# Another step table for the small stages of an attention, in a kernel of attention and mixture of experts

## The chip, the cores and the metric

The kernel runs on one core of one Trainium2 chip. The metric is the device time of one execution in microseconds (us), as the median of several runs. A core has five engines with an instruction queue each: TensorE (PE in the profile, matrix products and transposes by product; PEld is its weight load), VectorE (DVE), ScalarE (ACT), GpSimd (POOL) and SyncE (SP, which here only issues DMAs). Each engine works through its own queue in order; between engines there are semaphores.

## The reference

Eight batches of 512 tokens of width 512, all in fp32. Latent attention with 16 heads of 32, then routed and shared experts, each between two layer norms:

```python
x = x + layernorm(attention(layernorm(x)))
x = x + layernorm(ffn(layernorm(x)))
# attention: c_kv = x @ W_DKV + b, c_q = x @ W_DQ + b; k_c, v_c from c_kv, q_c from c_q
#            k = [k_c, rope(x @ W_KR)], q = [q_c, rope(x @ W_QR)]
#            ctx = softmax(q k^T / sqrt(32)) v_c; return ctx @ W_O + b_O
# ffn:       router (top 2 of 16 experts), routed relu^2 experts + shared relu^2 expert
```

## The kernel before

The kernel has four stages in a row: attention (to about 960 us), the first half of the shared expert with the routing beside it, the routed experts, and the second half of the shared expert with the combination. The change touches the attention alone.

**Units.** The attention is cut into 32 units `u`. A unit is four heads of one batch: `b = u // 4` is the batch, `g = u % 4` the group, so that each batch has a first (g = 0), second, third and fourth unit. For each unit PE makes 16 tiles of scores of 128 keys by 512 queries (`scores`, L598 and L603, two products into one PSUM bank); ACT takes the exponential of each (L1373) into a ring of eight tiles `K.pt`; PE multiplies four at a time with the values (`values`, L614); POOL adds the last twelve to the first four (`K.acc`, L1570) for the softmax's denominators. The maxima that the softmax needs are taken one unit ahead: PE makes 16 tiles of the next unit's products (`top`, L584) into three PSUM banks, DVE reduces each to its row maxima (L888), and when all 16 are reduced PE transposes them (`rows`, L590), which the next unit's scores need.

**Small stages.** After a unit's last values its context is kept (`keep`, ACT, L1380), `total` sums `K.acc` over partitions (PE, L623), `invert` transposes and inverts it (DVE, L895, L897, L900), `divide` multiplies the context with it (POOL, L1577), `round` makes the context's high part in fp32r (ACT, L1385), and `low` subtracts it from the context, which leaves the low part (DVE, L905, both operands in SBUF, 128x512). These six stages of unit u-1 stand in unit u. Beside them stand the halves of q and k two units ahead (`half`, then `send`, which passes them through DRAM, SP, L1719 to L1729), and by group: in the first unit the transposes of the next batch's input and the last batch's output projection (`project`, DVE L915), in the second the latent projections (`proj`) and the first norm of the last batch's output with four residual additions on POOL (L1604), in the third the rope projection and the second norm, in the fourth the values of the next batch, its norm, and the last batch's routing.

**What sets the order.** `beside_order(u)` gives each stage of a unit a step from 0 to 35 out of the table `STEP`; the sixteen scores stand at the even steps 0, 2, ... 30. All stages are sorted by `(32 * u + step, rank)`, and this one list is the order of instructions of every engine: each engine takes from it the stages that it has work in. There is no other planner. An engine that comes to a stage whose input is not there waits, and all that stands behind it in its queue waits too. Two numbers a stage in the table apart can thus stand close on one engine and far apart on another: `"round1": 24` and `"low1": 18` say that in a second unit DVE's subtraction stands at step 18 and the copy on ACT that it needs at step 24.

Of the kernel before, what the change touches and what calls it, by code (L numbers as in the profile page):

```python
# [137 lines left out]
def before_order(b):  # L138
    return ([("turn", b, k) for k in range(4)], [("proj", b, w) for w in ("kv", "q", "r")], [("v", b, i) for i in range(4)])


STEP = {"last values0": 9, "total0": 8, "invert0": 10, "divide0": 2, "round0": 14, "low0": 15, "k0": 1, "q0": 3, "rows0": 27,
# [10 lines left out]


def beside_order(u):
# [3 lines left out]
    def put(name, items):  # L159
        where = STEP[f"{name}{g}"]  # L160
        at.extend(((32 * u + n, 1), x) for n, x in zip(where if isinstance(where, tuple) else [where] * len(items), items))
# [9 lines left out]
    if u + 1 < NU:  # L171
        due = STEP[f"tops{g}"]
        for n in range(16):
# [1791 lines left out]
```

## Time and profile before

| | |
|---|---|
| three runs | 1722.57, 1723.14, 1726.42 us (median 1723.14) |
| the profiled execution | 1726.61 us, of which the span of the trace is 1724.8 |
| PE busy | 1581.1 us (92% of the span) |
| DVE, ACT, POOL busy | 986.8, 832.1, 795.4 us |
| attention, first exponential to last | 75.5 to 958.6 us |
| the four units of the fourth batch | 36.7, 24.1, 27.2, 28.1 us (second, third, fourth, then the first of the fifth) |

A row of the profile gives an engine, a line of the kernel, output and input by name, the form and how many there are, and behind the bar or in brackets for how long the engine was idle just before and who ended that. Names are those of the memory rooms: `a`, `s`, `c` and `f` are tiles in SBUF, `bank` is PSUM. Times of a timeline are us from the span's start.

### The profile page before, as it was taken

The numbers are of one execution on the slowest core, as the hardware profiler recorded it, in microseconds if no ns is written. First come the engines' busy times: TensorE is split into PE (matmuls) and PEld (weight loads), VectorE is DVE, ScalarE is ACT, GpSimd is POOL, SyncE is SP. The second block draws the span as 40 slices with busy tenths as digits, with TensorE's granted clock in tenths as the row PEclk, the third lists the DMA queues.
The fourth block names the chain that finished last, engine by engine and source line by source line (L and its number), as shares of the span: only waits on it lengthen the run. The fifth ranks groups of instructions, "written<-read, shape, count | busy, mean of one in ns | idle before, by whom it ended". The sixth has DMA issues, their size and how long they took to land.

```text
span 1724.8 us, 22216 instructions
## 1 busy us (share of the span) xinstructions
PE 1581.1 (92%) x7386; PEld 1078.2 (63%) x7386; DVE 986.8 (57%) x1896; ACT 832.1 (48%) x1496; POOL 795.4 (46%) x820
## 2 busy tenths in 40 slices
PE   4799979899899798998997899998999999979997
PEld 3465646556556465564563577887676767657886
DVE  3667677776766776767666442565111111128998
ACT  2356546465475464555654345430333333346554
POOL 1167767666677667666776440002222222122341
PEclk9799999899899899999998999997999999989999
DMA  4747457364384583653752325114833333367773
GB/s 119 209 127 204 113 142 238 98 195 142 122 241 116 138 250 98 180 157 122 214 178 91 122 73 190 48 39 145 317 126 131 126 131 127 118 233 249 231 244 129
DMA packets 123767, 270.57 MB, mean 157 GB/s; under 512 B 15396, under 2 KB 27044, under 8 KB 117508
## 3 DMA queue, kind: packets, MB, share of 16 engines
q1 hardware_dynamic: 97256, 205.97, 39.5%
q0 software_dynamic: 12912, 41.82, 7.6%
q10 hardware_dynamic: 13488, 21.37, 3.4%
q8 instruction: 61, 1.00, 0.2%
q14 instruction: 50, 0.41, 0.1%
HBM read 154.03 MB, written 92.01 MB: 143 GB/s over the span
## 4 chain that ended last, share of the span: by engine, by line
PE 73%; DVE 7%; DMA 7%; issue 5%; ACT 3%; SPq 3%; POOL 2%; DVEq 0%; POOLq 0%; ACTq 0%
PE bank L109 10%; PE bank L699 10%; PE bank L677 8%; PE bank L755 8%; PE bank L778 8%; PE bank L584 6%; PE bank L598 6%; PE bank L614 5%; PE bank L603 5%; DMA a<-kq_scratch 3%; PE bank L738 2%; SPq L1729 2%; DVE a L905 2%; DVE a L888 1%; DMA a<-in_L_attn_x 1%
## 5 line engine op out<-in xcount | busy, mean ns | idle before, releaser
L1570 POOL TENSOR_TENSOR a<-a 128x512 f32<-128x512 f32 x384 | 494.7, 1318 | 102.8 <-ACT a L1373 102.1
L1373 ACT ACTIVATE a<-bank 128x512 f32<-128x512 f32 x512 | 296.0, 597 | 246.0 <-PE bank L603 220.0
L888 DVE TENSOR_REDUCE a<-bank 128x1 f32<-128x512 f32 x512 | 323.3, 681 | 57.2 <-PE bank L584 55.8
L109 PE MATMUL bank<-a 128*128 128x512 f32 (+1 forms) x864 | 241.5, 402 | 6.1 <-DVE a L834 4.0
L598 PE MATMUL bank<-a 128*128 128x512 f32 x512 | 221.5, 433 | 4.6 <-ACT a L1373 4.6
L603 PE MATMUL bank<-a 68*128 68x512 f32 x512 | 205.6, 402 | 0.4 <-ACT a L1363 0.2
L584 PE MATMUL bank<-a 128*128 128x512 f32 x512 | 185.4, 431 | 22.0 <-DMA a<-kq_scratch 16.6
L677 PE MATMUL bank<-c 128*128 128x512 f32 x768 | 185.8, 401 | 19.3 <-ACT c L1425 11.4
L109 PEld LDWEIGHTS bank<-a 128*128 128x128 f32 (+1 forms) x864 | 161.5, 189 | 54.3 <-issue 10.3
L1639 POOL DMA_INDIRECT f<-h_scratch,f x79 | 74.8, 947 | 252.7 <-PE bank L738 230.0
L1211 DVE TENSOR_TENSOR f<-f 128x256 f32<-128x256 f32 x79 | 33.6, 425 | 267.9 <-ACT f L1497 267.9
L677 PEld LDWEIGHTS bank<-c 128*128 128x128 f32 x768 | 147.1, 193 | 56.3 <-issue 12.6
L699 PE MATMUL bank<-c 128*128 128x512 f32 x768 | 176.0, 389 | 2.1 <-ACT c L1440 1.6
L598 PEld LDWEIGHTS bank<-a 128*128 128x128 f32 x512 | 98.2, 192 | 107.5 <-issue 48.5
L699 PEld LDWEIGHTS bank<-c 128*128 128x128 f32 x768 | 143.9, 188 | 33.0 <-issue 2.2
L755 PE MATMUL bank<-f 128*128 x632 | 151.4, 383 | 0.2 <-issue 0.2
L584 PEld LDWEIGHTS bank<-a 128*128 128x128 f32 x512 | 98.4, 197 | 81.2 <-DVE a L888 23.0
L778 PE MATMUL bank<-f 128*128 x316 | 148.5, 593 | 0.0
L614 PE MATMUL bank<-a 128*32 128x512 f32 x1024 | 139.5, 627 | 0.0
L755 PEld LDWEIGHTS bank<-f 128*128 128x128 f32 x632 | 115.1, 192 | 13.6 <-issue 1.0
L905 DVE TENSOR_TENSOR a<-s,a 128x512 fp32r<-128x512 f32 x32 | 93.0, 2907 | 29.2 <-ACT a L1385 29.2
L603 PEld LDWEIGHTS bank<-a 68*128 68x128 f32 x512 | 98.4, 192 | 16.0 <-ACT a L1363 1.2
(186 smaller groups left out, 1904.5 us busy)
## 6 DMA issues: line engine op xcount, KB each, us to landing
a<-kq_scratch SPq DMA_DIRECT2D x192, 256.0 KB, 5.9
kq_scratch<-a SPq DMA_DIRECT2D x32, 1024.0 KB, 4.1
a<-a SPq DMA_DIRECT2D x80, 256.0 KB, 5.4
yp_scratch<-f ACTq DMA_DIRECT2D x79, 256.0 KB, 2.0
a<-in_L_attn_x SPq DMA_DIRECT2D x15, 1024.0 KB, 9.2
x_scratch<-a SPq DMA_DIRECT2D x8, 1024.0 KB, 5.2
h_scratch<-a SPq DMA_DIRECT2D x8, 1024.0 KB, 12.5
hT_scratch<-s SPq DMA_DIRECT2D x8, 1024.0 KB, 7.6
```

The lines of the kernel that those rows point to most:

```text
L109: t = e.matmul(out, a[n], b[n], start=n == 0 and m == 0, stop=n == len(ah) - 1 and m == 2)
L584: e.matmul(MX[n % 3][:], K.Qc[:, z, j, i * P:(i + 1) * P], K.Kc[:, z, j, :], start=True, stop=True).then_inc(Z.top, 1)
L598: e.matmul(SC[n % 2][:], K.Kc[:, z, j, i * P:(i + 1) * P], K.Qc[:, z, j, :], start=True, stop=False)
L603: e.matmul(SC[n % 2][:], K.KR[0:68, b % 2, j, i * P:(i + 1) * P], K.QR[0:68, u % 2, :], start=False, stop=True).then_inc(Z.score, 1)
L614: t = e.matmul(CT[HD * j:HD * j + HD, :], K.v[:, u % VS, i, HD * j:HD * j + HD], K.pt[:, n % NP, :], start=i == 0, stop=i == 3)
L677: t = e.matmul(bank[:], (K.sul if a else K.suh)[:, k, cut], (K.hTl if c else K.hTh)[:, k, :], start=m == 0, stop=m == 11)
L699: t = e.matmul(bank[:], (K.aTl if a else K.aTh)[:, k, cut], (K.sdl if c else K.sdh)[:, k, :], start=m == 0, stop=m == 23)
L755: t = e.matmul(K.UP[z][:, 0:FI], K.hTt[:, z, k * P:(k + 1) * P], K.flat[:, bass.ds(reg[i] + k * FI, FI)], start=k == 0, stop=k == 3)
L778: t = e.matmul(K.DN[z][:], K.eaT[:, z, k * P:(k + 1) * P], K.flat[:, bass.ds(reg[i] + 4 * FI + k * D, D)], start=k == 0, stop=k == 1)
L888: e.tensor_reduce(K.mx[:, i, j:j + 1], K.MX[n % 3][:], AX.X, ALU.max).then_inc(Z.max, 1)
L1373: e.activation(K.pt[:, n % NP, :], K.SC[n % 2][:], ACT.Exp, scale=SCALE).then_inc(Z.exp, 1)
L1570: e.tensor_tensor(K.acc[:, j, :], a, K.pt[:, n % NP, :], ALU.add).then_inc(Z.acc, 1)
```

## The change

86 of the table's 169 numbers change; nothing else is touched, so that each engine has the same instructions with the same operands, in another order. Of the table the rows of the second unit's low part:

```diff
-        "values0": (15, 15, 29), "tops0": (3, 4, 5, 6, 6, 7, 10, 11, 14, 14, 16, 16, 16, 16, 16, 16), "last values1": 7,
-        "total1": 7, "invert1": 7, "divide1": 8, "round1": 24, "low1": 18, "k1": 9, "q1": 11, "rows1": 30,
...
+        "values0": (16, 16, 31), "tops0": (3, 4, 5, 6, 6, 7, 9, 12, 15, 15, 16, 16, 16, 16, 16, 16), "last values1": 6,
+        "total1": 6, "invert1": 6, "divide1": 8, "round1": 14, "low1": 16, "k1": 8, "q1": 11, "rows1": 28,
```

The steps of `round` and `low` by group go from (14, 15), (24, 18), (17, 21), (23, 30) to (15, 16), (14, 16), (21, 30), (19, 27).

VectorE in unit 9 (the second unit of the third batch), from the second k half's low part (L875) to the latent projection of q (L847), before. L888 is a top's maximum, L905 the low part:

```order
L875 SCALAR_TENSOR_TENSOR a13<-bank5,a31,a13 128x512
L888 TENSOR_REDUCE a42<-bank2 128x1
L888 TENSOR_REDUCE a42<-bank3 128x1
L847 SCALAR_TENSOR_TENSOR a5<-bank6,a27,a4 128x512
L888 TENSOR_REDUCE a42<-bank4 128x1
L888 TENSOR_REDUCE a42<-bank2 128x1
L888 TENSOR_REDUCE a42<-bank3 128x1
L905 TENSOR_TENSOR a17<-s7,a23 128x512
L888 TENSOR_REDUCE a42<-bank4 128x1
L888 TENSOR_REDUCE a42<-bank2 128x1
L888 TENSOR_REDUCE a42<-bank3 128x1
L847 SCALAR_TENSOR_TENSOR a5<-bank5,a28,a4 128x512
```

The same stretch of VectorE after the change:

```order
L875 SCALAR_TENSOR_TENSOR a13<-bank5,a31,a13 128x512
L888 TENSOR_REDUCE a42<-bank4 128x1
L888 TENSOR_REDUCE a42<-bank2 128x1
L847 SCALAR_TENSOR_TENSOR a5<-bank6,a27,a4 128x512
L888 TENSOR_REDUCE a42<-bank3 128x1
L905 TENSOR_TENSOR a17<-s7,a23 128x512
L888 TENSOR_REDUCE a42<-bank4 128x1
L888 TENSOR_REDUCE a42<-bank2 128x1
L888 TENSOR_REDUCE a42<-bank3 128x1
L888 TENSOR_REDUCE a42<-bank4 128x1
L888 TENSOR_REDUCE a42<-bank2 128x1
L847 SCALAR_TENSOR_TENSOR a5<-bank5,a28,a4 128x512
```

The low part stood ahead of the last three maxima of the unit; now it stands ahead of the last six (five are shown, the sixth follows the last row).

ScalarE in the same unit, before. L1337 is the latent projection's eviction, L1316 the norm's scaling, L1373 an exponential, L1385 the rounding that the low part waits for:

```order
L1373 ACTIVATE a9<-bank1 128x512
L1337 ACTIVATE a4<-bank6,a27 128x512
L1316 ACTIVATE a43<-a43,a41 128x512
L1373 ACTIVATE a9<-bank0 128x512
L1373 ACTIVATE a9<-bank1 128x512
L1373 ACTIVATE a9<-bank0 128x512
L1373 ACTIVATE a9<-bank1 128x512
L1373 ACTIVATE a9<-bank0 128x512
L1385 CAST a23<-s7 128x512
L1373 ACTIVATE a9<-bank1 128x512
```

And after:

```order
L1337 ACTIVATE a4<-bank6,a27 128x512
L1373 ACTIVATE a9<-bank1 128x512
L1385 CAST a23<-s7 128x512
L1316 ACTIVATE a43<-a43,a41 128x512
L1373 ACTIVATE a9<-bank0 128x512
L1373 ACTIVATE a9<-bank1 128x512
L1373 ACTIVATE a9<-bank0 128x512
```

The rounding came behind the unit's thirteenth exponential; now it comes right behind the eighth (the L1373 above it), and the latent projection comes ahead of that exponential instead of behind it.

GpSimd from the division of unit 8's context in unit 9 (L1577) to the end of the unit, before. L1570 is an addition of exponentials, L1604 a residual addition:

```order
L1577 TENSOR_TENSOR s7<-s7,a21 128x512
L1604 TENSOR_TENSOR a44<-a43,a44 128x512
L1570 TENSOR_TENSOR a20<-a9 128x512 x3
L1604 TENSOR_TENSOR a44<-a43,a44 128x512 x2
L1570 TENSOR_TENSOR a20<-a20,a9 128x512 x3
L1604 TENSOR_TENSOR a44<-a43,a44 128x512
L1570 TENSOR_TENSOR a20<-a20,a9 128x512 x5
```

And after:

```order
L1577 TENSOR_TENSOR s7<-s7,a21 128x512
L1604 TENSOR_TENSOR a44<-a43,a44 128x512
L1570 TENSOR_TENSOR a20<-a9 128x512 x3
L1604 TENSOR_TENSOR a44<-a43,a44 128x512
L1570 TENSOR_TENSOR a20<-a20,a9 128x512
L1604 TENSOR_TENSOR a44<-a43,a44 128x512
L1570 TENSOR_TENSOR a20<-a20,a9 128x512 x2
L1604 TENSOR_TENSOR a44<-a43,a44 128x512
L1570 TENSOR_TENSOR a20<-a20,a9 128x512 x5
```

The third of the four residual additions moved behind the first L1570 that reads `a20` (the ninth tile's addition); the others stand where they stood.

VectorE at the end of unit 11, the fourth of its batch, after the change (before, L919, the routing's eviction, stood ahead of L905, and nothing else differs in these rows):

```order
L888 TENSOR_REDUCE a42<-bank4 128x1
L888 TENSOR_REDUCE a42<-bank2 128x1
L905 TENSOR_TENSOR a17<-s7,a23 128x512
L919 COPY lg<-bank5 128x64
L888 TENSOR_REDUCE a42<-bank3 128x1
```

## Rows read from the trace of the kernel before

**Rows 1.** The page, costliest groups: busy, mean ns | idle before, its releaser.
```profile
L905 DVE TENSOR_TENSOR a<-s,a 128x512 fp32r<-128x512 f32 x32 | 93.0, 2907 | 29.2 <-ACT a L1385 29.2
```
**Rows 2.** Windows, units 13 to 16: length, then busy time of each engine, granted clock.
```profile
423.90:460.60 36.70, 29.35 (x139) 18.59 (x138) 28.27 (x37) 16.51 (x29) 24.82 (x26) 0.89 0.40 115
460.60:484.70 24.10, 23.13 (x112) 13.13 (x111) 17.93 (x30) 14.88 (x26) 17.38 (x20) 0.96 0.47 128
484.70:511.90 27.20, 25.16 (x144) 16.12 (x143) 17.10 (x31) 19.26 (x34) 18.88 (x22) 1.00 0.87 260
511.90:540.00 28.10, 28.10 (x147) 18.81 (x146) 18.67 (x30) 13.32 (x25) 18.12 (x14) 1.00 0.55 154
```
**Rows 3.** Source L590 over the attention: what PE waited for before `rows`, us, times.
```profile
  DVE a L888: 54.5, 7
```
**Rows 4.** Timeline of PE at the end of unit 9: start, length, [idle before].
```profile
329.85 0.63 PE L109 MATMUL bank<-a 128*128 128x512 f32 x2
...
332.59 0.39 PE L598 MATMUL bank<-a 128*128 128x512 f32 x1
...
333.28 0.40 PE L603 MATMUL bank<-a 68*128 68x512 f32 x1
341.04 1.01 PE L590 MATMUL bank<-ident,a 128*4 128x128 f32 x4 [7.36 <-DVE a L888]
...
343.84 0.80 PE L598 MATMUL bank<-a 128*128 128x512 f32 x1
...
346.14 0.53 PE L598 MATMUL bank<-a 128*128 128x512 f32 x1
```
**Rows 5.** Timeline of DVE, same place.
```profile
330.48 8.61 DVE L905 TENSOR_TENSOR a<-s,a 128x512 fp32r<-128x512 f32 x1 [3.38 <-ACT a L1385]
339.02 1.87 DVE L888 TENSOR_REDUCE a<-bank 128x1 f32<-128x512 f32 x3
```
**Rows 6.** Source L905, all 32: least/median/greatest length in ns.
```profile
L905 DVE TENSOR_TENSOR a<-s,a x32: 691/1292/9670, 112.8 to 966.8; 128x512 fp32r<-128x512 f32 x32
```
**Rows 7.** Timeline of ACT in unit 9: seventh and eighth exponential, and the rounding.
```profile
321.23 1.08 ACT L1373 ACTIVATE a<-bank 128x512 f32<-128x512 f32 x2
323.34 0.69 ACT L1337 ACTIVATE a<-bank,a 128x512 fp32r<-128x512 f32 x1 [1.03 <-PE bank L109]
...
329.84 0.61 ACT L1385 CAST a<-s 128x512 fp32r<-128x512 f32 x1
```
**Rows 8.** Timeline of POOL, same unit.
```profile
321.16 3.78 POOL L1570 TENSOR_TENSOR a<-a 128x512 f32<-128x512 f32 x3
...
331.13 1.30 POOL L1604 TENSOR_TENSOR a<-a 128x512 f32<-128x512 f32 x1
332.38 6.17 POOL L1570 TENSOR_TENSOR a<-a 128x512 f32<-128x512 f32 x5
```
**Rows 9.** Timeline of PE at the end of unit 10, for PE's pace.
```profile
366.63 0.60 PE L590 MATMUL bank<-ident,a 128*4 128x128 f32 x4
...
368.15 0.50 PE L598 MATMUL bank<-a 128*128 128x512 f32 x1
...
370.66 0.98 PE L584 MATMUL bank<-a 128*128 128x512 f32 x3 [0.64 <-DMA a<-kq_scratch]
```
**Rows 10.** Timeline of DVE, the low parts in units 8 and 10.
```profile
292.28 1.22 DVE L905 TENSOR_TENSOR a<-s,a 128x512 fp32r<-128x512 f32 x1
...
362.64 1.32 DVE L905 TENSOR_TENSOR a<-s,a 128x512 fp32r<-128x512 f32 x1
```
**Rows 11.** Timeline of POOL around the first of these.
```profile
290.42 6.73 POOL L1570 TENSOR_TENSOR a<-a 128x512 f32<-128x512 f32 x5
```
**Rows 12.** Windows, unit 29 (second of the last batch), as in Rows 2.
```profile
883.90:920.00 36.10, 24.16 (x111) 13.41 (x110) 27.36 (x34) 14.77 (x26) 24.73 (x26) 0.86 0.47 145
```
**Rows 13.** Timeline of SP in unit 10: the sending of unit 12.
```profile
352.17 0.34 SPq L1719 DMA_DIRECT2D kq_scratch<-a  x1
358.44 0.60 SPq L1724 DMA_DIRECT2D a<-a  x1
```

More of the change, by code:

```diff
@@ L139, in before_order @@
     return ([("turn", b, k) for k in range(4)], [("proj", b, w) for w in ("kv", "q", "r")], [("v", b, i) for i in range(4)])
-STEP = {"last values0": 9, "total0": 8, "invert0": 10, "divide0": 2, "round0": 14, "low0": 15, "k0": 1, "q0": 3, "rows0": 27,
[10 rows of a table removed]
+STEP = {"last values0": 9, "total0": 8, "invert0": 10, "divide0": 9, "round0": 15, "low0": 16, "k0": 1, "q0": 2, "rows0": 27,
[10 rows of a table added]
 def beside_order(u):
```

16 rows, old and new, of the table STEP are left out of this document.

## The prediction

> **What bounds the kernel now.** The place to look first is the table of windows. In the attention PE is the engine that is busy nearly all the time: of the four windows [rows 2] the fourth is 28.10 us long with PE busy for all 28.10, the two in the middle lose 1.0 and 2.0 us, and the first, a second unit of a batch, is 36.70 us long with PE busy for 29.35. DVE, ACT and POOL are busy for 28.27 us or less in it, so no engine fills it: it holds a wait. The list of what PE waited for before `rows` says which: 54.5 us in seven waits on DVE's maxima [rows 3], one in each second unit but the first batch's. Six are like the one in unit 9: PE ends its last score at 333.7 and starts `rows` at 341.04, 7.36 us later [rows 4]; the seventh, in unit 29, is then 54.5 - 6 x 7.36 = 10.3 us.
>
> What DVE does meanwhile stands in its timeline: it waits 3.38 us for ACT's rounding (L1385), starts the low part L905 at 330.48, and that one instruction takes 8.61 us, to 339.09 [rows 5]. Three maxima follow, to 340.89, and PE goes on at 341.04. The page shows the same instruction 32 times with 93.0 us [rows 1]; the least is 0.69 us, the median 1.29, the greatest 9.67 [rows 6]. POOL tells what it waits for: from 321.16 on it has additions back to back; the last five start at 332.38 and end at 338.55 [rows 8]. L905 ends 0.54 us after that, so it got its turn when POOL's run ended. Both read two operands from SBUF.
>
> The wait has a second price. PE comes out of it at half its pace: four L590 and eight L614 take from 341.04 to 343.84, 2.80 us [rows 4], against 366.63 to 368.15, 1.52 us, in unit 10 [rows 9]. The next five products take 343.84 to 346.14, 2.30 us, against 1.14 by the twelve that take 329.85 to 332.59 (0.228 each) [rows 4]. The loss is 1.28 + 1.16 = 2.4 us. The granted clock in the windows agrees: 0.89 and 0.96 in the second and third unit, 1.00 in the other two [rows 2]. These are 1.2 and 2.4 GHz in turn, the lower after the idle time.
>
> **The change, part by part.** No instruction is added or removed; all is order.
>
> *The second unit's low part.* The rounding comes behind the eighth exponential instead of the thirteenth, the low part behind ten reduced maxima instead of thirteen. The latent projection now comes ahead of the eighth score, so that this exponential, which began about 321.8 [rows 7], comes 2.74 us later (twelve products [rows 4]); ACT takes the projection's eviction first (0.69 us [rows 7]), and I put the rounding's end at 308.3 + 16.2 = 324.5 and, with DVE's own two evictions ahead, the low part at 16.5 us into the unit, which begins at 308.3. Where is POOL then? Its additions five to seven began at 321.16 [rows 8], 12.8 us into the unit; the third of them is the one of the eighth exponential, and this now ends at 15.6 us. So POOL runs dry for a moment at 15.4, adds to 16.9, does one residual addition to 18.1, and the next addition needs the ninth exponential, which comes behind sixteen products of `values` (2 x 0.9 us, eight being 1.52 less four L590 [rows 9]) at about 18.2. A queue that is short when the low part comes is what the other units have: in unit 8 L905 came in the middle of an addition with others ready (290.42 to 297.15 without a break [rows 11]) and took 1.22 us, in unit 10 1.32 us [rows 10]. I take 1.3 us, between 0.69 (free) and 2.0 (two additions' ends, as far as the dry spot at 18.1). All is then done by 18.8 us, while `rows` comes at about 26. Price on the path: 0 us if PE gets its PSUM banks, up to 0.6 us if the tops behind step 18 catch up with DVE. I take 0.5.
>
> So 7.36 us of idle time and 2.4 us of half pace go in six units: 6 x 9.8 = 58.6 us. What is late next? POOL: nine additions and three residuals after 15.6 us take 12 x 1.25 = 15.0 us, with the low part's 0.5 to 31.1, while the unit now ends at 36.7 - 9.3 = 27.4. It then ends 3.7 us into the third unit; `total` needs it there at about 4.3. That is 0.6 us of cover, so this costs nothing, or 1 to 2 us where I am off by that.
>
> *Unit 29*, the last batch's, has 36.10 us with 24.16 us of PE [rows 12]. 10.3 + 2.4 = 12.7 us go from PE, but POOL has 24.73 us of work in it [rows 12], against 24.82 in a unit that is five us longer for PE [rows 2]. POOL ends some 6.5 us into unit 30, where `total` stands at 4, and the backlog passes on to the end of unit 31. I count 9.5 us saved and 3.2 given back.
>
> *The other three low parts* go one step later (first unit), from 21 to 30 (third) and from 30 to 27 (fourth). In the third it stands behind all maxima of the unit, and the next thing on DVE is the next unit's: even a wait for POOL's whole run, to 25.5 us, would be hidden, since PE itself waits there for a DMA (0.64 us here, 370.66 [rows 9]). In the fourth it comes at about 19.6 us, next to the norm's eight small POOL steps. I take no cost for all three; the upper bound is a rival below.
>
> *Halves of k and q* go earlier (third unit 4, 5 to 1, 2). SP shows that this buys nothing: it writes them at 352.17 but issues the copy that needs the rope part (L1724) only at 358.44 [rows 13], and the rope's projection goes from step 9 to 10. With a third unit that is 0.5 to 0.7 us shorter, the wait at 370.66 grows by about that: 0.6 us a batch given back, 6 x 0.6 = 3.6. *Projections, norms, QR copies* change places in a first unit without idle time; their cost I put at 0, and 0 to 1 us a batch as the bound.
>
> **A rule of the skill, weighed.** The trace shows L905 at 8.61 us across six POOL instructions [rows 5, 8]. The Trainium skill, "SBUF — State Buffer", "Who interferes with whom", says that a DVE instruction with two SBUF inputs contends with a GpSimd instruction that reads SBUF, and that the second to issue waits until the first has finished, for one instruction. By that rule as I read it the wait would be 1.3 us at most and the table would have nothing to gain here; the trace does not agree. The same page says in its summary that deep queues would have to be drained for sharing. By that any low part in a run of additions would wait for the end of the run; the trace agrees in unit 9 and not in unit 8.
>
> **The sum.** 58.6 + 9.5 = 68.1 us, less 6 x 0.5 for the tops and 3.6 for the DMA: 61.5 us. Against the profiled execution's 1726.6 us that is 1665.1. That execution lies 3.5 us above the median of the three runs, so the median after is 1723.1 - 61.5 = 1661.6; I say 1661.
>
> **Rivals.**
>
> *A. The fourth unit's low part meets a run* (the rule on drained queues, as a mechanism of this kernel). At 19.6 us POOL has the norm behind it and seven additions ahead; if the low part waits for the last of them, at about 29.8, DVE is 2.9 us late in the next first unit. PE stops at its fourth top: 2.5 to 3 us, seven times, 17 to 21 us. Time: 1680. For it: the long waits all ended with a run; against it: half of the 32 took 1.29 us or less [rows 6] although POOL had additions without a break at most of them, as in unit 8 [rows 10, 11]. The Trainium skill, the same section, bears on this one.
>
> *B. Still refused in the second unit: slower.* If the low part at 16.5 us is not let in at 16.9 and the ninth exponential comes a little before 18.1, POOL does not run dry, and the run goes on to 31.2 us. Now six maxima stand behind the low part, not three: PE stops at its fourteenth top, about 19.6 us into the unit, and has 27.4 - 19.6 = 7.8 us of work left. The unit is 31.2 + 7.8 = 39.0 us long instead of 36.7, seven times: +16 us, time 1739. It decides at the ninth exponential: 0.1 us ahead of POOL's residual addition. Against it: in unit 8, a short case, the next addition but one waited for its exponential, and here too POOL has one instruction ready or none behind the one that runs.
>
> *C. POOL bounds the second unit.* If its additions end 2 to 3 us later than I count, `total` waits for them and PE with it: +1.5 to 2.5 us seven times, 1675.
>
> *D. No change that counts.* The stall goes, but others of the 86 moved numbers give it all back in the units with no idle time now. Nothing in the rows speaks for it: 1720 to 1726.
>
> **Chances.** The forecast 0.72, A 0.11, B 0.07, C 0.07, D 0.03. The forecast's own spread: up to 2.0 us a batch less (low parts, POOL's cover) gives 1675; the 20 us of PE idle time outside the seven waits, of which a better order could take half, gives 1648. Two thirds of A and all of C lie below 1684, so the range 1647 to 1684 leaves out B, D and the rest of A, and something for what I have not seen: about 2 in 10. What a measurement can tell is about 0.2%, 3.4 us. Faster by more than that: 0.90; within: 0.03; slower: 0.07.
>
> **What would show it.** Right: L905 in second units at 2 us or less; no wait before L590 on DVE of more than 1 us; their windows at 27.4 to 28.5 us; the granted clock at 1.00 from 230 us on in all windows; the third unit's total under 24 us. Wrong: a long L905 anywhere (A in the fourth unit, B in the second, with PE's wait before L584 in place of L590); PE waiting before L623 in third units for POOL (C); DMA waits at the start of the fourth unit of 3 us or more, since all waits on SP's order were taken as they are.

## The result, and the profile after

The kernel with the new table takes **1656.2 us** (median, 1654.3 to 1658.7) against 1724.8 us for the kernel before on the same chip (1722.6 to 1727.8). The ratio is **0.960**, with a 95% interval of 0.958 to 0.963: 68.6 us less, where 61.5 had been forecast. The profiled execution took 1658.7 us, with a span of 1656.9.

The units that the prediction was about come first. The windows of the kernel after, in the columns of [rows 2] (length, busy time of PE, PEld, DVE, ACT, POOL, granted clock, DMA share, GB/s): units 13 to 15, then 29 and 30.

```profile
403.70:430.90 27.20, 26.91 (x135) 17.75 (x135) 20.67 (x37) 15.93 (x27) 22.60 (x25) 1.00 0.50 144
430.90:453.20 22.30, 22.14 (x112) 12.44 (x111) 15.77 (x29) 14.86 (x26) 20.45 (x22) 1.00 0.53 151
453.20:482.70 29.50, 27.21 (x146) 17.68 (x145) 17.87 (x32) 18.60 (x34) 19.01 (x22) 0.94 0.83 241
823.50:846.00 22.50, 22.50 (x111) 13.07 (x109) 17.86 (x31) 14.65 (x25) 18.33 (x21) 1.00 0.40 116
846.00:870.00 24.00, 19.95 (x96) 10.90 (x96) 15.62 (x25) 13.51 (x24) 23.14 (x26) 0.93 0.48 154
```

The second unit is down from 36.70 us [rows 2] to 27.20, and PE is busy for 26.91 of them. Unit 29 is down from 36.10 [rows 12] to 22.50, with PE busy throughout. The third window, a fourth unit, has grown from 27.20 [rows 2] to 29.50, and its granted clock is 0.94; that clock was not forecast.

The seven waits of [rows 3] are gone; of the two on DVE that are left, one (1.1 us) stands ahead of the first unit, as it did before, and the other, in unit 13, is 0.2 us long. What PE waits for ahead of `rows` (L590) in the kernel after, us and times ("issue": nothing that the profile shows), and the low part, least/median/greatest length in ns, as in [rows 6]:

```profile
  issue: 6.1, 24
  DVE a L888: 1.3, 2
```
```profile
L905 DVE TENSOR_TENSOR a<-s,a x32: 681/926/6856, 106.5 to 897.1; 128x512 fp32r<-128x512 f32 x32
```

Unit 9 in the timeline: ACT's rounding, DVE's low part, and POOL's work around it (start, length).

```profile
314.46 0.62 ACT L1385 CAST a<-s 128x512 fp32r<-128x512 f32 x1
```
```profile
315.46 1.03 DVE L905 TENSOR_TENSOR a<-s,a 128x512 fp32r<-128x512 f32 x1
```
```profile
312.11 3.83 POOL L1570 TENSOR_TENSOR a<-a 128x512 f32<-128x512 f32 x3
315.90 1.73 POOL L1604 TENSOR_TENSOR a<-a 128x512 f32<-128x512 f32 x1
317.59 1.29 POOL L1570 TENSOR_TENSOR a<-a 128x512 f32<-128x512 f32 x1
```

The low part is asked for at 315.46, POOL's instruction ends at about 315.9, and the low part is over at 316.49: 1.03 us where it took 8.61 [rows 5]. POOL's next instruction, begun at 315.90, takes 1.73 us instead of 1.30 [rows 8]: it now waits for DVE, by 0.4 us, and not DVE for it. POOL adds on without a break until 330.10.

**Where the time went.** Taking a unit from its first exponential to the next unit's, over the six batches that have all four (units 4 to 27), the mean lengths are:

| | before | after | difference |
|---|---|---|---|
| first unit | 28.02 | 28.13 | +0.11 |
| second unit | 36.69 | 26.98 | -9.71 |
| third unit | 23.67 | 22.30 | -1.37 |
| fourth unit | 26.74 | 27.49 | +0.75 |
| six batches | 690.7 | 629.4 | -61.3 |
| units 29 to 31, to the first product of L677 | 84.0 | 74.7 | -9.3 |

The rest of the program adds 2.7 us, which makes the -67.9 us between the two spans (1724.8 and 1656.9).

**What was not forecast.** Fourth units begin with a wait of PE for the loads of k and q: 0.99 to 2.29 us. The wait itself is not new: in the kernel before it was 0.64 to 2.13 us, and the mean over the six batches is 1.36 us in both. New is what follows it: in units 15 and 27 PE goes on at half pace. Here is the longest wait, in unit 15: PE, and SP's queue in the unit before.

```profile
456.57 1.45 PE L584 MATMUL bank<-a 128*128 128x512 f32 x3 [2.29 <-DMA a<-kq_scratch]
457.81 0.63 PE L598 MATMUL bank<-a 128*128 128x512 f32 x1
...
461.23 0.40 PE L584 MATMUL bank<-a 128*128 128x512 f32 x1
```
```profile
435.09 0.34 SPq L1719 DMA_DIRECT2D kq_scratch<-a  x1
442.92 0.60 SPq L1724 DMA_DIRECT2D a<-a  x1
444.22 3.85 SPq L1729 DMA_DIRECT2D a<-kq_scratch  x6
```

The projected halves are written to the scratch buffer at 435.09. The loads from it (L1729) are issued only at 444.22, because the two copies of the rotated rows (L1724, L1725) stand ahead of them in SP's queue and wait for the next batch's rotation. The loads land after PE is ready for them. After the 2.29 us, PE is at half pace, and products come back to 0.40 us long at about 461. In the kernel before, the same wait in unit 15 had no half pace behind it (three products in 0.97 us, here 1.45), nor had the one of 2.13 us in unit 19:

```profile
487.82 0.97 PE L584 MATMUL bank<-a 128*128 128x512 f32 x3 [2.04 <-DMA a<-kq_scratch]
```

The other long thing left is one low part, in unit 30:

```profile
867.02 6.86 DVE L905 TENSOR_TENSOR a<-s,a 128x512 fp32r<-128x512 f32 x1
```
```profile
863.36 9.97 POOL L1570 TENSOR_TENSOR a<-a 128x512 f32<-128x512 f32 x8
```

It ends 0.55 us after POOL's eight additions have ended, like the waits of the kernel before. No PE wait hangs on it.

### The profile page after: what moved, and what is told of

It reads as the page before. It is cut to its first block, busy times and chain, and to the rows that moved or that the text cites. A ratio compares the mean times of both kernels' runs of the same rounds, so it can differ in the third digit from the quotient of the medians.

```text
span 1656.9 us, 22215 instructions
## 1 busy us (share of the span) xinstructions
PE 1569.0 (95%) x7386; PEld 1079.2 (65%) x7386; DVE 926.2 (56%) x1896; ACT 829.9 (50%) x1496; POOL 799.4 (48%) x820
## 4 chain that ended last, share of the span: by engine, by line
PE 82%; DMA 7%; ACT 2%; DVE 2%; SPq 2%; issue 2%; POOL 1%; DVEq 0%; ACTq 0%; POOLq 0%
PE bank L109 13%; PE bank L699 10%; PE bank L677 9%; PE bank L755 8%; PE bank L778 8%; PE bank L598 7%; PE bank L584 6%; PE bank L603 6%; PE bank L614 6%; DMA a<-kq_scratch 4%; PE bank L738 2%; PE bank L623 2%; SPq L1729 2%; PE bank L727 1%; DMA kq_scratch<-a 1%
## 5 line engine op out<-in xcount | busy, mean ns | idle before, releaser
L1570 POOL TENSOR_TENSOR a<-a 128x512 f32<-128x512 f32 x384 | 496.0, 1320 | 153.1 <-ACT a L1373 92.9
L1373 ACT ACTIVATE a<-bank 128x512 f32<-128x512 f32 x512 | 297.5, 598 | 245.9 <-PE bank L603 198.7
L888 DVE TENSOR_REDUCE a<-bank 128x1 f32<-128x512 f32 x512 | 323.6, 681 | 54.6 <-PE bank L584 53.5
L677 PE MATMUL bank<-c 128*128 128x512 f32 x768 | 188.9, 406 | 18.5 <-ACT c L1425 11.6
L677 PEld LDWEIGHTS bank<-c 128*128 128x128 f32 x768 | 149.1, 196 | 56.2 <-issue 12.4
L614 PE MATMUL bank<-a 128*32 128x512 f32 x1024 | 131.9, 600 | 0.0
L1507 ACT COPY f<-bank 128x512 f32<-128x512 f32 x79 | 46.3, 585 | 122.2 <-PE bank L778 122.2
```

The lines of the kernel that those rows point to most:

```text
L614: t = e.matmul(CT[HD * j:HD * j + HD, :], K.v[:, u % VS, i, HD * j:HD * j + HD], K.pt[:, n % NP, :], start=i == 0, stop=i == 3)
L677: t = e.matmul(bank[:], (K.sul if a else K.suh)[:, k, cut], (K.hTl if c else K.hTh)[:, k, :], start=m == 0, stop=m == 11)
L888: e.tensor_reduce(K.mx[:, i, j:j + 1], K.MX[n % 3][:], AX.X, ALU.max).then_inc(Z.max, 1)
L1373: e.activation(K.pt[:, n % NP, :], K.SC[n % 2][:], ACT.Exp, scale=SCALE).then_inc(Z.exp, 1)
L1570: e.tensor_tensor(K.acc[:, j, :], a, K.pt[:, n % NP, :], ALU.add).then_inc(Z.acc, 1)
```

## The experiments

"Kept out" means in what follows that the low part, once asked for, is not let in at the end of the POOL instruction that runs then, but only at the end of a run of them; "the port" is a short word for that wait and no more.

Theory 1 throughout: the low part, asked for in a run of POOL's additions, is kept out until the run ends; this, and the half pace behind PE's wait, is what the table removes. Theory 2: another of the 86 numbers, or the rounding's lateness alone, makes the difference. Each kernel was timed beside the kernel before.

**e1_round_low.** The kernel before with two numbers of the new table.

```diff
-"round1": 24, "low1": 18,
+"round1": 14, "low1": 16,
```

> The table of before with two numbers of the change alone: the second units' rounding at step 14 and low part at 16. Theory (the long low part and the half pace behind it are the gain): second units of about 27.5 us instead of 36.7, L905 at 1.0 to 2.0 us there, no wait before L590 of more than 1 us, and 60 us less than before, 1660 to 1668 us. Rival (the gain is spread over many of the 86 numbers): less than half of the 68 us, so above 1690.

Measured: 1659.8 us (1658.9 to 1664.6), ratio 0.962 (0.960 to 0.964). Two numbers carry 65 of the 68.6 us. The mean second unit is 27.63 us, the third 23.14. Two low parts are still kept out in it, of 3.63 and 4.27 us, neither in a second unit. The first, in unit 7, a fourth unit, is rival A's case: DVE comes late into unit 8, PE waits there for a maximum, and unit 8 takes 29.93 us where the other first units take 27.6 to 28.1. DVE, then PE:

```profile
269.62 3.63 DVE L905 TENSOR_TENSOR a<-s,a 128x512 fp32r<-128x512 f32 x1
```
```profile
273.91 0.50 PE L584 MATMUL bank<-a 128*128 128x512 f32 x1 [1.59 <-DVE a L888]
```

**e2_round_only.** Of these two numbers only the rounding's, so that the low part stays behind the thirteenth maximum.

```diff
-"round1": 24,
+"round1": 14,
```

> The table of before with the rounding of second units at step 14 alone; the low part stays at step 18, and comes to DVE at about 18.8 us into the unit, in the middle of GpSimd's run of additions, with one or two of them ready. Theory 1 (a low part is let in at the next addition's end while at most two GpSimd instructions stand ready behind it, and waits for the run's end only with three or more): L905 at about 1.3 us, second units of 27 to 28 us, 1660 to 1670 us. Theory 2 (any low part in an unbroken run of additions waits for its end): L905 from 18.8 to about 30.7 us, 10 us and more, second units of 39 us or more, slower than before by 10 to 20 us. Theory 3 (only the late rounding matters, 3.4 us of wait on ScalarE): L905 stays at 8 us or so, and the time falls by 20 us or less.

Measured: 1695.1 us (1688.9 to 1711.9), ratio 0.984 (0.976 to 0.992), a wide spread. One trace shows both outcomes in the same kind of unit. DVE and POOL in units 5 and 9, and PE in unit 5:

```profile
212.30 12.12 DVE L905 TENSOR_TENSOR a<-s,a 128x512 fp32r<-128x512 f32 x1
...
327.32 0.98 DVE L905 TENSOR_TENSOR a<-s,a 128x512 fp32r<-128x512 f32 x1
```
```profile
210.20 2.55 POOL L1604 TENSOR_TENSOR a<-a 128x512 f32<-128x512 f32 x2
212.70 3.79 POOL L1570 TENSOR_TENSOR a<-a 128x512 f32<-128x512 f32 x3
216.44 1.30 POOL L1604 TENSOR_TENSOR a<-a 128x512 f32<-128x512 f32 x1
217.68 6.18 POOL L1570 TENSOR_TENSOR a<-a 128x512 f32<-128x512 f32 x5
```
```profile
325.20 2.55 POOL L1604 TENSOR_TENSOR a<-a 128x512 f32<-128x512 f32 x2
327.69 4.24 POOL L1570 TENSOR_TENSOR a<-a 128x512 f32<-128x512 f32 x3
```
```profile
226.36 1.01 PE L590 MATMUL bank<-ident,a 128*4 128x128 f32 x4 [7.42 <-DVE a L888]
```

In unit 5 the low part is asked for 0.40 us before POOL's next instruction and is kept out for all nine that follow, 12.12 us. In unit 9 it is asked for 0.37 us before the next one, in the same order of instructions, and is let in. Four second units (5, 13, 17, 25) went the first way, with 36.4 to 36.8 us each, two (9, 21) the second, with 27.5. So a low part inside the run can cost all or nothing. The distance to POOL's next instruction does not tell the two apart: it was 0.399, 0.378, 0.399 and 0.379 us in the four that were kept out, 0.372 and 0.379 us in the two that were let in. This is also rival B's mechanism, seen on the chip: refused early, the low part takes longer (12.1 us) than it did before (8.6).

**e3_undo_in_after.** The reverse: the new table with the old two numbers.

```diff
-"round1": 14, "low1": 16,
+"round1": 24, "low1": 18,
```

> The table of after with the second units' rounding and low part put back to 24 and 18. Theory: the long low part is back, 8 to 9 us in the seven second units, with PE idle for 7 us before L590 and half pace behind it: 55 to 75 us above after, 1712 to 1731 us. Rival (the other 84 numbers make the gain as well): less than 30 us above after.

Measured: 1706.6 us (1702.0 to 1712.0), ratio 0.991 (0.988 to 0.993). The loss is there, 50 us against the kernel after, but I had its form wrong. Unit 9, ACT, DVE and PE:

```profile
331.52 0.63 ACT L1385 CAST a<-s 128x512 fp32r<-128x512 f32 x1
```
```profile
332.18 1.66 DVE L905 TENSOR_TENSOR a<-s,a 128x512 fp32r<-128x512 f32 x1 [4.94 <-ACT a L1385]
```
```profile
332.04 0.40 PE L603 MATMUL bank<-a 68*128 68x512 f32 x1
336.44 1.01 PE L590 MATMUL bank<-ident,a 128*4 128x128 f32 x4 [4.01 <-DVE a L888]
337.11 0.77 PE L598 MATMUL bank<-a 128*128 128x512 f32 x1
```

The low part takes 1.66 us, not 8 or 9. But DVE stands for 4.94 us at its head for a rounding that comes late, and the last maxima of the unit are queued behind it; PE waits 4.01 us for them and comes out at half pace (the next product 0.77 us long for 0.40). The mean second unit is 32.78 us: 5.8 us over the kernel after. So in the new table the late rounding alone (theory 2's part) costs several us a unit. That does not hold for the kernel before, as e4 will show: there the rounding stands at step 24 too, but the second projection at 27 and not at 21, ahead of it, and `rows` at 30 and not at 28; the rounding ends 22.1 us into the unit (24.0 here), and PE is ready for `rows` at 25.4 (24.3 here). Kept out were two low parts only, in unit 29 (9.51 us) and, as in the kernel after, in unit 30.

**e4_small_additions.** The kernel before, in its own order, with POOL's run made short.

```diff
+        if i > 1:
+            e.tensor_tensor(K.acc[:, j, 0:64], K.acc[:, j, 0:64], K.pt[:, n % NP, 0:64], ALU.add).then_inc(Z.acc, 1)
+            return
```

> The kernel before with GpSimd's additions of exponentials from the ninth tile on cut from 512 columns to 64 (the rest of each is left out of the computation); every instruction and every wait stays in its place. Theory 1 (it is the standing run of 512-column additions that keeps the low part at L905 out of its memory port): the additions now take a few tenths of a us, so the low part is in within 1.0 us everywhere, PE waits under 0.5 us ahead of the projections at L590 in second units, these units fall from 36.7 to about 27 us, and the time goes to 1650 to 1665 us, without any change of order. Theory 2 (the place in the order is wrong by itself: the rounding is ready too late whatever GpSimd does): second units stay over 32 us and the time over 1700.

Measured: 1660.6 us (1657.8 to 1662.1), ratio 0.961 (0.959 to 0.964). L905 in it:

```profile
L905 DVE TENSOR_TENSOR a<-s,a x32: 681/692/1532, 113.5 to 899.7; 128x512 fp32r<-128x512 f32 x32
```

With nothing moved, no low part is longer than 1.53 us, and the time is 4 us from the new table's. The rounding is as late as before; DVE, then PE, in unit 13:

```profile
427.50 0.69 DVE L905 TENSOR_TENSOR a<-s,a 128x512 fp32r<-128x512 f32 x1 [3.38 <-ACT a L1385]
```
```profile
430.29 0.40 PE L603 MATMUL bank<-a 68*128 68x512 f32 x1
430.52 0.60 PE L590 MATMUL bank<-ident,a 128*4 128x128 f32 x4
```

DVE still waits 3.38 us for it, and PE waits for nothing: the second units take 27.48 us. Only in unit 29 does PE wait, 2.22 us. So theory 1 holds for the kernel before, and theory 2 does not: POOL's run was what kept the low part out, and the lateness of the rounding was covered. What the edit can't tell is whether it is the length of the additions or that they stood without a break that mattered, since it changes both.

**e9_low_on_gpsimd.** The new table, with the low part itself on POOL; the same function leaves VectorE's list of stages and enters GpSimd's.

```diff
+    def low(u):
+        g = u % NG
+        w.wait_ge(Z.cx_hi, u + 1)
+        e.tensor_tensor(K.cxl[:, g, :], K.cx[:, g, :], K.cxh[:, g, :], ALU.subtract).then_inc(Z.cx_lo, 1)
```

> The kernel after with the low part's subtraction given to GpSimd, at the same place of the step table. Nothing is left at L905 on VectorE, so nothing can be refused there. Theory 1 (the whole gain is that the low part no longer waits for GpSimd's run to end; the port is all there is to it): time within -6 to +12 us of after (1650 to 1668), since GpSimd takes one more instruction of about 1.2 us a unit, and the low part stands behind whatever of its additions is queued: one or two, 1.3 us each. Rival (GpSimd then bounds the second unit, since its additions come late to the total): second units over 28.5 us, and a time over 1670.

Measured: 1677.5 us (1676.4 to 1681.7), ratio 0.972 (0.970 to 0.975), outside theory 1's range, and over the rival's 1670, but for another reason than the rival's. Second units are as good as in the kernel after (26.93 us mean). First units are not: 30.89 us instead of 28.13. POOL and PE in unit 8:

```profile
280.24 5.00 POOL L1570 TENSOR_TENSOR a<-a 128x512 f32<-128x512 f32 x4
285.18 1.28 POOL L1582 TENSOR_TENSOR a<-s,a 128x512 fp32r<-128x512 f32 x1
```
```profile
286.61 3.01 PE L109 MATMUL bank<-a 128*128 128x512 f32 x12 [1.92 <-POOL a L1582]
```

The low part (L1582 here) stands in POOL's queue behind four additions, and PE waits 1.92 us for it, in unit 28 2.30 us. In units 12, 20 and 28 half pace follows. The move frees DVE of the port and puts the same run ahead of the low part by another way: a queue.

**e6_low_at_22** and **e7_low_early_in_others.** The new table, with the low part at other places.

```diff
 (e6)
-"low1": 16,
+"low1": 22,
 (e7)
-"low2": 30,  "low3": 27,
+"low2": 22,  "low3": 20,
```

> The kernel after with the low part of a batch's first unit at 22 instead of 16, the rounding still at 14, so that VectorE comes to it later, with other work of its own between the two. Theory 1 (let in at the first end of a GpSimd instruction, or else only when its queue is empty; which of the two depends on how many additions are ready then): in second units the low part is either about 1 us or 8 to 12 us long with nothing between; if long, PE waits at L590 and the time is 1690 to 1725 us. Rival (GpSimd lets it in at one of its next instructions' ends whatever is queued): never over 3 us, time 1655 to 1662.

> The kernel after with the low parts of the third and fourth units nearer to their roundings (low2 from 30 to 22, low3 from 27 to 20). Theory 1 (what decides is whether the request meets an end of a GpSimd instruction that lets it in, or is held until GpSimd's queue is empty): these two get lengths of 0.7 to 2 us or of 4 to 9 us and nothing between; if both stay short, the time is that of after, 1653 to 1660 us. Rival (PE gains from an earlier low part in these units too): 1645 to 1652 us; the trace of after has no wait of PE ahead of L590 in them, so I expect no gain.

Measured: e6, timed once, 1659.6 us; e7 1654.8 us (1652.2 to 1659.2), ratio 0.959 (0.957 to 0.961), not to be told from the kernel after. No low part was kept out in e7 (greatest 1.75 us), and in e6 none but the one in unit 30 that the kernel after has too (6.82 us). In e6 second units lose 1.0 us each (27.99): the low part, 1.15 us long, is asked for 1.0 us before PE is ready for `rows`, with the last maximum behind it, and PE waits 0.92 us. So with the rounding early, the low part's place is cheap at 22 in this table; at 18 in the old one (e2) it cost 9 us in four units of six. And e6 shows a request that a deep queue did not keep out. Unit 29 in it, DVE and POOL:

```profile
845.40 0.68 DVE L905 TENSOR_TENSOR a<-s,a 128x512 fp32r<-128x512 f32 x1
```
```profile
844.24 1.28 POOL L1570 TENSOR_TENSOR a<-a 128x512 f32<-128x512 f32 x1
845.47 1.74 POOL L1604 TENSOR_TENSOR a<-a 128x512 f32<-128x512 f32 x1
847.18 2.52 POOL L1570 TENSOR_TENSOR a<-a 128x512 f32<-128x512 f32 x2
```

By the times of their inputs five POOL instructions were ready when this low part was asked for, and it was let in after 0.07 us. My rule of a queue that must be short falls with it.

**e5_send_first.** SP's loads ahead of the copies of rotated rows, in every send of the kernel after: the first try at the fourth unit's wait.

```diff
-        w.wait_ge(Z.rope, 3 * (b + 1))
-        e.dma_start(raw(K.Kc[96:128, z, :, :]), rep(0)).then_inc(Z.stack[z], 16)
-        e.dma_start(raw(K.Qc[96:128, z, :, :]), rep(32)).then_inc(Z.stack[z], 16)
...
             e.dma_start(raw(t[HD * k:HD * k + HD, z, :, :]), piece(n)).then_inc(Z.stack[z], 16)
+        w.wait_ge(Z.rope, 3 * (b + 1))
+        e.dma_start(raw(K.Kc[96:128, z, :, :]), rep(0)).then_inc(Z.stack[z], 16)
+        e.dma_start(raw(K.Qc[96:128, z, :, :]), rep(32)).then_inc(Z.stack[z], 16)
```

> After, with the order of SP's issues in a send changed: the six loads of the halves from DRAM first, then the wait for the rope part and its two copies. Theory (the fourth unit's first top waits for loads that stand behind the wait for the rope part): PE's 21.2 us of waits on DMA before L584 fall to under 6 us, and the three stretches at half pace behind them go as well: 10 to 20 us less than after, about 1641. Rival (the rope copies themselves land last and are the wait): 0 to 5 us less.

Measured: 1672.4 us (1671.5 to 1675.7), ratio 0.970 (0.968 to 0.971): 16 us slower than the kernel after. Fourth units do what was expected (25.63 us for 27.49), but third units go from 22.30 to 25.65. PE at the start of unit 6:

```profile
227.77 0.96 PE L584 MATMUL bank<-a 128*128 128x512 f32 x3 [1.44 <-DMA a<-a]
```

Now it is the copies (a<-a) that land last. In three sends of four the rotation is long done, the copies wait for nothing, and they fit into the time in which SP waits for the halves to reach the scratch buffer; behind the loads they come late.

**e8_loads_ahead_once.** So the order is turned only in the one send of four whose copies wait for a new rotation; `copies` is the wait and the two copies that e5 moves.

```diff
+        late = u % NG == 0 and u >= NG
...
+        if not late:
+            copies()
...
+        if late:
+            copies()
```

> The kernel after, with SyncE's loads put ahead of the copies of the rotated rows in the one send of four that is issued in a batch's first-unit slot (send of unit 4, 8, ..., 28), the others as they were. Theory 1 (fourth units begin with a wait for weights whose load stood behind the copies' wait in the queue, and with e5 the loss came from the other three sends): whichever send it is, the 1.0 to 2.3 us at the start of fourth units go only if that load is the late one; if so 1640 to 1652 us. Theory 2 (the late load belongs to another send, or the copies in this one are just as pressed): the waits at the start of fourth units stay and the time is 1656 +- 4, or it is some us slower where the copies now come last.

Measured: **1645.0 us** (1642.9 to 1645.6), ratio **0.953** (0.951 to 0.955), the fastest kernel of the study. SP in the unit before unit 15, and PE at its start:

```profile
429.88 0.34 SPq L1719 DMA_DIRECT2D kq_scratch<-a  x1
433.84 2.69 SPq L1735 DMA_DIRECT2D a<-kq_scratch  x6
437.72 0.60 SPq L1727 DMA_DIRECT2D a<-a  x1
```
```profile
448.85 0.93 PE L584 MATMUL bank<-a 128*128 128x512 f32 x3
```

The loads go as soon as the halves are in the scratch buffer, 3.96 us after these were sent (9.13 us in the kernel after), and PE has no wait. Fourth units fall to 25.62 us, third ones stay at 22.26. Of the spans' difference to the kernel after, 13.1 us, the six batches make 11.2. The kernel before has the same wait, and the same edit was not tried on it.

**e10_earlier_send.** e8 with the halves, and the send behind them, earlier in second units; what is left of DMA waits in e8 is 3.84 us at the start of unit 30.

```diff
-"k1": 8, "q1": 11,
+"k1": 4, "q1": 6,
```

> e8 with the weights' halves of the unit after next four and five steps earlier in second units (k1 from 8 to 4, q1 from 11 to 6), and with them the send behind them. What is left of PE's waits in e8 is 3.84 us at the start of unit 30, for the loads of the send that is issued 12 us into unit 29. Theory 1 (that send is late because its halves are): it is issued some 3 us earlier, the 3.84 us fall to about 1 us, and nothing else moves: 1638 to 1643 us. Theory 2 (the halves, put ahead of the division's matmuls, hold up ACT's and DVE's additions of the bias, and these the rounding and the tops): second units grow by 0.3 to 1 us each, 1645 to 1652 us.

Measured: 1652.5 us (1652.0 to 1658.4), ratio 0.958 (0.956 to 0.961), 7 us slower than e8. The wait in unit 30 falls to 1.76 us, but second units grow to 28.20 us. PE in unit 13:

```profile
412.67 0.50 PE L584 MATMUL bank<-a 128*128 128x512 f32 x1 [0.58 <-DVE a L888]
```

The invert and the divide come 1.4 and 1.7 us later behind the halves; that is theory 2 of its expectation, with 1.2 us a unit where it had at most 1. It also holds the one low part in these traces that was refused at one end and let in at the next, DVE and POOL in unit 30:

```profile
861.95 1.85 DVE L905 TENSOR_TENSOR a<-s,a 128x512 fp32r<-128x512 f32 x1
```
```profile
855.76 12.90 POOL L1570 TENSOR_TENSOR a<-a 128x512 f32<-128x512 f32 x10
```

## Why the prediction was right, point by point

- **The bound and the cause** were read rightly: PE idle behind one DVE instruction, and that behind POOL. e4 shows the cause apart from any move, e1 shows that the two numbers named are the change.
- **The second unit**, six times 9.8 us forecast (7.36 idle, 2.4 half pace), measured 9.71 in the second and 1.37 in the third unit, 11.1 together and 66.5 for 58.6. e1, which moves the two numbers alone, gives the term by itself: 9.1 in the second and 0.5 in the third unit, 9.6 in all, of which 7.3 us are idle time of PE and 2.3 are half pace, part of it paid in the third unit. So the term was right in size. The rest of the 11.1 is the other 84 numbers: third units lost a wait of 0.7 us for DVE's maxima, which e1 and e4 still have, and some of PE's work moved out of the second unit.
- **The DMA term** was wrong: 0.6 us a batch was to be given back in the wait that [rows 9] shows with 0.64 us. It stands at the start of fourth units, and its mean is 1.36 us before and 1.36 after. Fourth units did grow, by 0.75 us, but by PE's busy time: some 0.5 us is the half pace in units 15 and 27, the rest is work that stood elsewhere before. That 0.75 is near 0.6 is luck.
- **The sum.** 61.5 us were forecast and 67.9 measured between the profiled spans. The six batches gave 61.3 us for 52.0 forecast (3.0 for the tops and 3.6 for the DMA were not given back, and 2.7 more came), the last three units 9.3 for 9.5, and the rest of the program took 2.7 us back, for which the forecast had no term. In the spread, half of 20 us below 1661 is 1651 and not 1648.
- **The low part's place**: forecast at 16.5 us into the unit and 1.3 us long; measured 15.8 and 1.03. The 0.5 us a unit for tops behind it were not needed: PE is idle for 0.09 to 0.29 us in these units. They take 26.9 to 27.2 us, just under the 27.4 to 28.5 named as the sign.
- **What is late next**: POOL's additions end 3.5 us into the third unit (3.7 forecast) and cost nothing there. Rival C did not happen.
- **Unit 29**: 9.5 us forecast for the last three units, 9.3 measured; 13.7 gained in unit 29 and 5.4 given back in unit 30. What PE waits for there is not POOL's backlog, as forecast, but a send, with half pace behind it:

```profile
849.74 1.65 PE L584 MATMUL bank<-a 128*128 128x512 f32 x3 [3.73 <-DMA a<-kq_scratch]
```

  The backlog is there too, behind that wait: POOL's additions end 7.8 us into unit 30 (6.5 forecast) and `total` starts 0.3 us after them. So the loads alone would not have given the time back; in e10 the wait is 2.1 us shorter and unit 30 is no shorter. The size was right, and in part for another cause than the one given.

- **Other low parts**: no cost, as taken. In fourth units 1.1 to 1.7 us, asked for 20.3 to 23.2 us into the unit, where rival A would have had 10; e7 moves it and changes nothing. By the letter of its own signs ("a long L905 anywhere") the one of 6.86 us in unit 30 speaks against the forecast; it cost nothing. Rival A's mechanism exists: e1 has it once, at the price of 1.9 us.
- **A mis-said sign**: "the granted clock at 1.00 in all windows from 230 us on". It is 0.94 in units 15 and 27 and 0.93 in unit 30, each time behind a wait for a DMA.
- **What carried luck**: the place of the request was worked out, but not why it would be let in. I argued from a short queue, with a dry spot of POOL at 18.1 us as the second chance. There was no dry spot: the ninth exponential ended 17.6 us into the unit, before POOL's residual addition did (18.0), and POOL ran on to 30.5 us. That is the condition of rival B; only that the low part was let in at the first end, in all six units, kept B away. e6 shows one let in with five ready, and e1 two kept out with one and one ready. Over the ten traces with L905 on DVE and POOL's work whole, 21 of 320 low parts were kept out, each until 0.55 us after the last of a run of additions (0.547 to 0.556 in all 21), and the other 299 took 0.68 to 1.85 us. The prediction's chance of 0.07 for B was low for what e2 showed: four of six such units refused, at the same distance as the other two. What decides at the end of a POOL instruction stays open; e10's case shows that a first refusal is not always final.

The Trainium skill, "SBUF — State Buffer", "Who interferes with whom", has the second to issue blocked until the first finishes. Read as a wait for one instruction, the traces contradict it: 8.61 us [rows 5] and 12.12 us across six and nine POOL instructions. The 298 low parts that were never refused agree with it: none waited past the end of the POOL instruction that ran. (The sentence on deep queues that the prediction cites stands in that page's section "SBUF: two separate sides", not in its summary.) In the other direction the traces agree: one POOL instruction behind the low part, in unit 9 of the kernel after, ends 0.4 us late, and the next takes its usual 1.29 us.

## What to carry to other kernels

A DVE instruction with two SBUF operands beside a run of GpSimd additions has two prices here, about 0.7 to 1.7 us or the rest of the run, and a kernel may get either with the same order and the same timing: give it slack for the longer one, or make its input early enough that the run's end comes before anyone needs it. When a step waits on its engine, ask separately what the wait for its input costs and what the wait to be let in costs, and ask it in the table at hand: a rounding at step 24 cost next to nothing in the old table (e4) and 50 us in the new one (e3). And in a DMA queue, look for the one issue whose wait is new: turning the order in that send alone gained 11 us, turning it in all of them lost 16. The wait stood in the profile of the kernel before as well, where a forecast could have priced it.

## What the runs showed of the hardware

- A refused request is not served at a later end of a POOL instruction, with one exception in 22 (e10, at the second end), although up to nine ends pass. It is served 0.55 us after POOL's last addition. POOL's instruction behind the refusal takes its usual 1.26 to 1.31 us, the one behind a low part that was let in 1.71 to 1.78.
- Whether a request is refused goes with its distance to the start of POOL's next instruction, but not alone. Of the 283 low parts asked for inside a run, the 22 refused ones were at 0.01 to 0.07, 0.35 to 0.40, 0.52 to 0.53, 0.64 to 0.66 and 1.22 to 1.24 us; in the first four of these bands 10 others were let in, and outside the five, 251 of 251. This is read off afterwards; no run tested it, and why it is so is open.
- The same gap of PE has two outcomes. 2.29 us and 1.45 us in the kernel after were followed by half pace (the next product 0.59 and 0.75 us long for 0.40, the ones behind it 0.63), 2.04 and 2.13 us in the kernel before were not. What it cost beyond its own length: PE is busy for 27.21 us in the window of unit 15, and for 25.7 in the fourth units without half pace: 1.5 us.
- Maxima from PSUM (L888) and the norm's statistics, with one SBUF operand (L816), were never held: at most 0.70 us for the latter over 96, beside the same runs of additions.
